# Row sums of P taken from a GpSimd addition of its key tiles, in both 32-wide attentions of an eight-stage kernel

## The reference, cut to what matters

```python
scores = einsum('bqkgd,bskd->bkgqs', q, k) * 32 ** -0.5
scores = where(causal, -inf, scores)
P      = softmax(scores, axis=-1)          # exp(s - max) / sum over the keys
out    = einsum('bkgqs,bskd->bqkgd', P, v)
x      = x + out @ Wo
```

## Time and profile before

| | us |
|---|---|
| median of 3 runs | 4135.32 (4134.88 to 4137.27) |
| profiled execution, its own time | 4134.45 |
| span of the profiled execution | 4132.6 |
| PE busy in the span | 3217.2 (78%) |
| POOL busy in the span | 563.8 (14%) |

### The profile page before, as it was taken

The page is one execution under the profiler, slowest core; times in us unless marked ns, Lnnn a source line. Parts: engine busy times, 40 slices in busy tenths (PEclk is TensorE's granted clock), DMA queues, the critical chain, the costliest instruction groups (busy, mean ns, idle before and its releaser), DMA issues. The chain is left out here.

```text
span 4132.6 us, 52343 instructions
## 1 busy us (share of the span) xinstructions
PE 3217.2 (78%) x19426; PEld 2419.0 (59%) x19426; DVE 1970.5 (48%) x4588; ACT 1126.1 (27%) x2319; POOL 563.8 (14%) x713
## 2 busy tenths in 40 slices
PE   6999899989999558888781888768787876006999
PEld 5777688867666334556661666356565654005887
DVE  4444432134443453135756666355556564994111
ACT  2223311113322102112220222133333344772000
POOL 0010132211100000001310000021212121001222
PEclk8999899988999768899995999889898988557999
DMA  2000200010000302120001000300000002000000
GB/s 75 2 2 2 88 1 0 1 49 2 2 1 1 105 1 82 41 87 1 0 3 79 0 0 0 102 1 2 1 2 1 2 1 85 0 0 0 11 11 21
DMA packets 45111, 88.97 MB, mean 22 GB/s; under 512 B 6723, under 2 KB 10307, under 8 KB 44229
## 3 DMA queue, kind: packets, MB, share of 16 engines
q1 hardware_dynamic: 44454, 85.60, 5.9%
q0 software_dynamic: 416, 0.10, 0.0%
HBM read 81.60 MB, written 4.19 MB: 21 GB/s over the span
## 5 line engine op out<-in xcount | busy, mean ns | idle before, releaser
L602 DVE CUSTOM_DVE_ANT_0 bank<-bank,a_causal 128x384 f32<-128x384 f32 (+3 forms) x512 | 235.9, 524 | 156.1 <-PE bank L711 156.1
L95 PE MATMUL bank<-f_xT_hi,f_w_hi 128*128 128x512 f32 (+1 forms) x704 | 276.2, 392 | 5.7 <-DVE f_w_lo L1081 4.1
L96 PE MATMUL bank<-f_xT_hi,f_w_lo 128*128 128x512 f32 (+1 forms) x704 | 275.7, 392 | 0.0
L97 PE MATMUL bank<-f_xT_lo,f_w_hi 128*128 128x512 f32 (+1 forms) x704 | 275.5, 391 | 0.0
L527 ACT ACTIVATE a_PT<-bank 128x512 f32<-128x512 f32 (+1 forms) x384 | 174.4, 526 | 238.1 <-PE bank L724 237.9
L1130 PE MATMUL bank<-ident,f_xn 128*128 128x128 f32 x128 | 18.4, 306 | 282.6 <-DVE f_xn L1069 282.6
L897 ACT ACTIVATE bank<-f_bit,f_lut,f_step 128x512 f32<-128x512 int32 x264 | 190.7, 767 | 85.7 <-DVE bank L934 47.6
L1130 PEld LDWEIGHTS bank<-ident,f_xn 128*128 128x128 f32 x128 | 17.2, 160 | 284.3 <-DVE f_xn L1069 283.5
L1101 DVE TENSOR_TENSOR f_sg<-bank,f_sg 128x512 f32<-128x512 f32 (+1 forms) x44 | 30.4, 691 | 286.9 <-PE bank L97 286.9
L2175 PE MATMUL bank<-a_KT,a_QT 128*128 128x256 f32 (+1 forms) x512 | 144.0, 390 | 20.2 <-ACT a_QT L1972 20.2
L1099 DVE SCALAR_TENSOR_TENSOR f_sg<-bank,f_us,f_sg 128x512 f32<-128x512 f32 x44 | 33.0, 751 | 264.2 <-PE bank L97 264.2
(11 more groups left out here) (441 smaller groups left out, 8394.0 us busy)
## 6 DMA issues: line engine op xcount, KB each, us to landing
f_w_raw<-in_f_w SPq DMA_DIRECT2D x11, 768.0 KB, 13.1
f_idx<-in_f_idx SPq DMA_DIRECT2D x11, 768.0 KB, 12.4
x_res<-in_x SPq DMA_DIRECT2D x4, 1024.0 KB, 9.5
m_piece<-in_m_wq SPq DMA_DIRECT2D x2, 2048.0 KB, 11.5
m_piece<-in_m_wo SPq DMA_DIRECT2D x2, 2048.0 KB, 9.4
m_piece<-in_m_w_gate SPq DMA_DIRECT2D x2, 2048.0 KB, 10.9
m_piece<-in_m_w_up SPq DMA_DIRECT2D x2, 2048.0 KB, 7.8
m_piece<-in_m_w_down SPq DMA_DIRECT2D x2, 2048.0 KB, 11.1
```

The costliest lines, as they stand in the source:

```text
L95: pe.matmul(out, w[0], x[0], start=first, stop=False, skip_group_check=True)
L96: pe.matmul(out, w[1], x[0], start=False, stop=False, skip_group_check=True)
L97: return pe.matmul(out, w[0], x[1], start=False, stop=last, skip_group_check=True)
L602: last = dve.tensor_tensor_reduce(out=ps[J.bank(key)][:, col:col + n], in0=ps[J.bank(key)][:, col:col + n], in1=causal[:, T - n:T], scale= ...
```

## The change

The sum over keys is taken in two steps. POOL first adds the key tiles of P into a new tile `added` of 128 x 4 x 512: once the tiles f = 0 to 7 are there, a copy of 128 columns per head (A1), an addition of 384 columns per head (A2) and one of 128 (A3); once f = 8 to 11 are there, an addition of 256 (A4). The letters A1 to A4 are names of this text. PE then needs one product for each query tile and head, 16 in all. They form an entry `sums` of their own in chunk 1 of the next unit, and `bc` moves from chunk 1 to chunk 2. At a sequence's end `sums` stands in the middle of `qkv`. ACT waits, before it overwrites a `PT` tile, for the POOL addition that reads it. V has one buffer in place of two.

```diff
-    V = [prog.sb(f"{name}_V{i}", [P, TT, KC * P], F32) for i in range(2)]
+    V = prog.sb(name + "_V", [P, TT, KC * P], F32)
+    added = prog.sb(name + "_added", [P, G, T], F32)
...
                 if k == 1 and u >= 1:
+                    ORDER.append(("sums", (b, u - 1), 0))
+                if k == 2 and u >= 1:
                     ORDER.append(("bc", (b, u - 1), 0))
...
             ORDER.append(("pv", end, 2))
-            ORDER += [("qkv", b + 1, i) for i in range(len(QKV))] + [("bc", end, 0)]
+            ORDER += [("qkv", b + 1, i) for i in range(len(QKV) // 2)] + [("sums", end, 0)]
+            ORDER += [("qkv", b + 1, i) for i in range(len(QKV) // 2, len(QKV))] + [("bc", end, 0)]
...
+                elif kind == "exp" and k >= 2:
+                    n = 4 * unit(at)
+                    for f in range(8) if k == 2 else range(8, 12):
+                        pool.wait_ge(*read(("exp", at, f)))
+                    if k == 2:
+                        if n:
+                            before = unit(at) - 1
+                            pool.wait_ge(*full(("sum", (before // DC, before % DC))))
+                        pool.tensor_copy(added[:, :, 0:P], PT[0][:, :, 0:P]).then_inc(c_added.sem, 1)
+                        pool.tensor_tensor(added[:, :, P:T], PT[0][:, :, P:T], PT[1][:, :, 0:3 * P], ALU.add).then_inc(c_added.sem, 1)
+                        pool.wait_ge(*c_added(0, n + 2))
+                        pool.tensor_tensor(added[:, :, 3 * P:T], added[:, :, 3 * P:T], PT[1][:, :, 3 * P:T], ALU.add).then_inc(c_added.sem, 1)
+                    else:
+                        pool.wait_ge(*c_added(0, n + 3))
+                        pool.tensor_tensor(added[:, :, 2 * P:T], added[:, :, 2 * P:T], PT[2][:, :, :], ALU.add).then_inc(c_added.sem, 1)
...
                             act.wait_ge(*pv_done((before // DC, before % DC), j))
+                            act.wait_ge(*c_added(0, 4 * before + j + 2))
...
-                    for col, kt in T_PARTS[k]:
-                        for qt in range(kt, TT):
-                            for g in range(G):
-                                strip = slice(HD * g, HD * (g + 1))
-                                at_ = col + (qt - kt) * P
-                                last = pe.matmul(ps[J.bank(key_s)][strip, 0:P], sums[:, qt, :], PT[k][:, g, at_:at_ + P],
-                                                 start=kt == 0 and qt == 0, stop=kt == 2, skip_group_check=True)
...
+                elif kind == "sums":
+                    key = ("sum", at)
+                    pe.wait_ge(*vacant(key))
+                    pe.wait_ge(*c_added(0, 4 * unit(at) + 4))
+                    for qt in range(TT):
+                        for g in range(G):
+                            last = pe.matmul(ps[J.bank(key)][HD * g:HD * (g + 1), 0:P], sums[:, qt, :], added[:, g, qt * P:(qt + 1) * P],
+                                             start=qt == 0, stop=qt == TT - 1, skip_group_check=True)
```

More of the change, by code:

```diff
@@ L371, in attention32 @@
         else:
-            ORDER += [("pv", end, 2), ("bc", end, 0)] + [("Y", b, k) for k in range(4)]
+            ORDER += [("pv", end, 2), ("sums", end, 0), ("bc", end, 0)] + [("Y", b, k) for k in range(4)]
     jobs = [("const", 7)] if biased else []
@@ L385, in attention32 @@
         elif kind == "pv" and k == 0:
-            jobs += [(("O", at), O_BANK), (("sum", at), SUM_BANK)]
+            jobs.append((("O", at), O_BANK))
+        elif kind == "sums":
+            jobs.append((("sum", at), SUM_BANK))
         elif kind == "bc":
@@ L401, in attention32 @@
     c_qk, c_nm, c_nm_hi, c_nm_lo, c_pv = (prog.count(n) for n in ("qk_hi", "nm", "nm_hi", "nm_lo", "pv"))
+    c_added = prog.count("added")
     c_ot_hi, c_ot_lo = (prog.count(n) for n in ("ot_hi", "ot_lo"))
@@ L410, in pv_done @@
     def pv_done(at, j):
-        return full(("sum", at)) if j == 2 else c_pv(0, 2 * unit(at) + j + 1)
+        return full(("O", at)) if j == 2 else c_pv(0, 2 * unit(at) + j + 1)
     with nc.Block() as block:
@@ L505, in _ @@
                     if what == "V":
-                        act.activation(V[at % 2][:, c, :], ps[J.bank(key)][:, 0:KC * P], ACT.Copy).then_inc(J.frees(key), 1)
+                        act.activation(V[:, c, :], ps[J.bank(key)][:, 0:KC * P], ACT.Copy).then_inc(J.frees(key), 1)
                         continue
@@ L623, in _ @@
                         normalise(at[0] + 1)
-                elif kind == "pv" and k == 2:
+                elif kind == "sums":
                     key = ("sum", at)
@@ L735, in _ @@
                     b, c = at
-                    key, key_s = ("O", at), ("sum", at)
+                    key = ("O", at)
                     if k == 0:
                         pe.wait_ge(*vacant(key))
-                        pe.wait_ge(*vacant(key_s))
                         if c == 0:
@@ L747, in _ @@
                             strip = slice(HD * g, HD * (g + 1))
[L748 removed]
+                            v = V[:, kt, (c % KC) * P + HD * g:(c % KC) * P + HD * (g + 1)]
                             last = pe.matmul(ps[J.bank(key)][strip, kt * P:T], v, PT[k][:, g, col:col + (TT - kt) * P],
                                              start=kt == 0, stop=kt == 2, skip_group_check=True)
[L751 to L760 removed]
+                    last.then_inc(J.fills(key) if k == 2 else c_pv.sem, 1)
+                elif kind == "sums":
+                    key = ("sum", at)
[5 more added lines that the diff above has]
+                                             start=qt == 0, stop=qt == TT - 1, skip_group_check=True)
+                    last.then_inc(J.fills(key), 1)
                 elif kind == "bc":
@@ L802, in attention32 @@
     c_nm_lo.advance(NB * DC)
+    c_added.advance(4 * NB * DC)
     c_pv.advance(2 * NB * DC)
```

1 line of the change is left out of this document (removed).

## The result

The changed kernel takes **4268.41 us** (median of 4 runs, 4265.39 to 4273.92) against 4135.48 (4 runs), a ratio of 1.0322 with a 95% interval of 1.0304 to 1.034. That is 133 us slower; 39 were forecast, and the range ended at 4198. The direction was right, the size and the main cause were not.

The account below looks back on a forecast made before the run. PE was taken as the bound (78% busy), with DVE and ACT close behind. Savings of 9.6 and 16.8 us against waits, late work and clock loss summed to +39.2 on a 4132.6 us span, giving 4174 us; range 4145 to 4198.

Parts of the forecast that it names:

- the same within 0.2 us per sequence: Casts of xT at sequence ends: counting DVE's port contention with POOL leaves the summed cost unchanged within 0.2 us per sequence.
- The clock term: Before `qkv`, six PE waits: the clock falls to half afterwards, costing 2.7 us each, +16.2 us.
- -9.6 for 16 steady units: Units 1 and 2 at full clock: 0.6 us gained each, all in chunk 3; chunk 0 and the middle nothing.
- -16.8 for unit 0: Eight units 0, largely at half clock: fewer products save 2.1 us each, in chunks 2 and 3.
- the line for POOL's additions: POOL's additions: 2.1 ns per column plus 0.2 us, giving A2 3.42, A3 1.27, A4 2.35; A1 0.61 us.
- the late casts of xT: Sequence ends: POOL's additions delay the casts and so `qkv`, +14.8 us in `a0` and +5.1 in `a1`.
- PE waits for `added` in units 1 of `a1`: POOL's additions to x in unit 0 delay A4, so PE waits 2.8 us, four times: +11.2 us.
- +2.0 forecast: Steady units of `a0`: POOL's chain ends late, so PE waits 0.25 us at `sums`, eight times.
- The end of `a0`: Behind the last unit no `qkv` covers POOL's additions, so the reciprocal starts later: +6.2 us.
- POOL's speed: Two rivals on POOL's additions: slower than the line, 4196 to 4205 us, chance 0.13; at one-input rate, 4122, chance 0.05.
- the clock at one place: Rival: the clock does not fall, or only for a moment, at the six waits before `qkv`; 4158 us, chance 0.2.
- gains and waits that cancel: Rival for the whole kernel: nothing comes of the change; 4135 us, chance 0.07.

Follow-up runs that it names:

- Run 1: The changed kernel with DVE's normalise of the next sequence moved behind the maxima of chunk 1 of unit 2, when POOL is idle: 4218.32 us.
- 13: 5 with A2 in two halves, the second only after DVE has written L for the next unit, and normalise one chunk later: 4206.56 us.
- 9: 5 with one wait more: POOL begins all of A2 only when DVE has written L for the next unit: 4239.43 us.
- 5: The changed kernel with normalise moved, casts of xT ahead of unit 3's additions, and `a1`'s additions to x early, right behind those: 4171.36 us.
- run 7: The changed kernel with POOL's additions stubbed to two-column copies (sums left out) and additions to x right behind the casts of xT: 4134.74 us, ratio 1.0009.
- 10: 9 with the last unit of each attention taking its row sums directly from P with the 40 products, without additions: 4232.16 us.
- 14: 13 with the last unit of each attention taking its row sums directly from P, as before the change: 4198.06 us.

## Why the prediction was wrong

- **The failed step is contention.** The prediction read DVE's slowing beside POOL from one instruction, L564, and closed with "the same within 0.2 us per sequence". It never asked which other DVE instructions lie in SBUF alone and stand where POOL now works. Two groups do, and both are on PE's path: normalise (L554) and the pair L616 and L618, taken at their old 1.92, 0.18 and 0.19 us. They measured 6.05, 1.29 and 0.19. Run 1 puts 50 us on the first. For the pair PE waits 1.30 us in a steady unit, which takes 15.51 us against 14.41 in the best unit of 13; the gain of all 32 could not be had, as 9 and 13 show.
- **The clock term** was put at six waits before `qkv`, 16.2 us, and these ends came out at +41.2 for +42.0. That is not luck: `qkv` starts 5.2 us later in `a0` and 2.05 in `a1` (4.9 and 1.7 forecast), and what follows is 19.5 us longer in sum (22.1 forecast), with waits of up to 7.5 us. The mechanism was right, and applied in too few places: the units 2 with their waits of 2.6 to 4.7 us for `max` have it too, 13.7 to 17.1 us at half clock in each of the six. Waits of 1.3 us alone mostly left the clock up, as in the steady unit above; in 5 one such unit fell (19.6 us). PE's busy time says how large it is in all: +48.5 us, where the products gone should have given back 33 (1.04 in each of 32 units, by a steady one: 14.90 and 13.86) to 47 (1.5 in each, the prediction's price).
- **-9.6 for 16 steady units** was 0.6 each. Chunk 3's 0.6 came in run 7 (0.61), but chunk 0, put at nothing, lost 0.2 and the middle 0.14, so 0.3 without contention. With the pair beside A2 it is +0.6.
- **-16.8 for unit 0** was twice too much (-8.6): in run 7, with fewer products and no additions, it was -6.1, and the clock comes back later there (137.6 us at half clock in the eight units 0, where 113.6 were before).
- **Right:** the line for POOL's additions (3.42, 1.27, 2.35, 0.61 forecast; 3.46, 1.30, 2.38, 0.61 measured), POOL's busy time, the late casts of xT and the price of sequences' ends. **Half right:** PE waits for `added` in units 1 of `a1`, but 4.5 us in all and not 11.2, since PE itself comes late there. In the units of `a0` it never waits for it (+2.0 forecast). The end of `a0` cost 10.5 for 6.2, 5.2 of it PE's wait for `added`.
- **The rivals** were about POOL's speed, the clock at one place, and gains and waits that cancel. None had POOL's work making DVE slow, though the prediction had a row of it and quoted a rule for it; that was the rival with the largest price. What it quoted names DVE instructions with two SBUF inputs, which L618 has; normalise and L616 have one tensor as input (`x_res`, `mx`), and they were slowed most.

**Still open.** 5 stands at 4171 and 7 at 4135; of these 37 us the pair has up to 1.1 in each of some 20 units, the stages' last units 7 to 8.5 (runs 10, 14), and the rest would be falls of the clock; the sum is an argument, not shown by a run of its own. Nor is it told apart whether in 7's units 0 the clock comes back later because PE has less to do or because of the short waits that took their place. And 7 was not run without its one collision in `a1`.

## What to carry to other kernels

Before work is put on POOL, list every DVE instruction whose operands all lie in SBUF and that would run beside it, however small, and price each as "until POOL's instruction ends" (1.1 us for one of 0.18 here), then what PE does in that time and the clock behind it. Work taken from an engine that is 100% busy is worth only what the next engines' ends leave: test the saving with the new work stubbed out first, for here that was 4134.7 against 4130.7, and some 7.5 less at best: no gain to pay for anything.

## What was not expected of the hardware

- Shorter POOL instructions didn't help a pair of DVE instructions here: with A2 in four, DVE's two took 0.76 and 0.92 in place of 1.29 and 0.19 us. DVE comes in between two of POOL's, one instruction at a time.
- One-input casts and copies of POOL hold DVE up like additions (L639 0.50 for 0.18 us beside a cast, an instruction of normalise 1.25 for 0.54 beside a copy), and it goes both ways: beside normalise POOL's cast took 0.80 for 0.61 and A4 2.53 for a mean of 2.38.
- In run 7, with 24 products fewer in a unit and `sums` and `bc` one chunk later, PE was at half clock for 248 us in place of 186, 19 of the 62 in the one unit with a collision.
